# Edge weights scaled in PSUM a group ahead, in place of gathered rows scaled at their landing

## What is computed

```python
h = jax.nn.silu(edge_length_embedded @ W_fc1 * (1.0 / math.sqrt(N_BASIS)))
w = h @ W_fc2 * (1.0 / math.sqrt(N_HID))
w1, w2, w3, w4 = (w[:, 0 * MUL:1 * MUL], w[:, 1 * MUL:2 * MUL], w[:, 2 * MUL:3 * MUL], w[:, 3 * MUL:4 * MUL])
x0s = y0[edge_src]
x1s = y1[edge_src]
ea0 = edge_attr[:, :1]
ea1 = edge_attr[:, 1:]
mid0a = w1 * x0s * ea0
mid0b = w4 * jnp.einsum('eum,em->eu', x1s, ea1) * (1.0 / math.sqrt(3.0))
mid1a = (w2 * x0s)[:, :, None] * ea1[:, None, :]
mid1b = w3[:, :, None] * x1s * ea0[:, None, :]
edge_features = jnp.concatenate([mid0a, mid0b, mid1a.reshape(E, -1), mid1b.reshape(E, -1)], axis=1)
agg = jax.ops.segment_sum(edge_features, edge_dst, num_segments=N)
```

## Time and profile before

| | us |
|---|---|
| median of 3 runs | 4927.12 |
| lowest, highest | 4906.59, 4927.83 |
| span of the profiled execution | 4361.2 |
| tensor pass in it, first gather to last sums | 116.8 to 1278 |
| busy in the whole span: PE, DVE, ACT, POOL | 3150.7, 2326.6, 1273.1, 2831.6 |
| mean granted TensorE clock | 0.861 |

### The profile page before, as it was taken

One profiled execution on the slowest core, in us unless ns is written; L12 is line 12 of the kernel. 1 busy time (PEld: TensorE's weight loads), 2 busy tenths in 40 slices (PEclk: granted clock), 3 DMA queues, 4 the chain that ended last, 5 costly groups with the idle time before them and its releaser, 6 DMA issues. The chain is left out here.

```text
span 4361.2 us, 67130 instructions
## 1 busy us (share of the span) xinstructions
PE 3150.7 (72%) x22048; PEld 2138.5 (49%) x22049; DVE 2326.6 (53%) x7490; ACT 1273.1 (29%) x2767; POOL 2831.6 (65%) x2851
## 2 busy tenths in 40 slices
PE   2677777777677888764534457987888688886886
PEld 1666665666555555432322244555555455554444
DVE  5677777777655666666657772335232432324223
ACT  1334344444434444434332240003111121112112
POOL 2777776666534767546747756764777577774775
PEclk8899999999988998975555568998999899997998
DMA  5324455667963444304444558764888578885876
GB/s 181 85 68 96 76 97 91 90 101 102 119 125 88 121 117 116 93 22 85 80 93 79 99 102 266 243 205 156 266 265 262 168 247 263 262 265 168 263 242 181
DMA packets 470576, 659.32 MB, mean 151 GB/s; under 512 B 108665, under 2 KB 335266, under 8 KB 469462
## 3 DMA queue, kind: packets, MB, share of 16 engines
q1 hardware_dynamic: 356438, 377.29, 34.7%
q0 software_dynamic: 113792, 277.69, 24.2%
HBM read 542.27 MB, written 112.46 MB: 150 GB/s over the span
## 5 line engine op out<-in xcount | busy, mean ns | idle before, releaser
L1716 POOL DMA_INDIRECT pass_rows<-table_sage,src_idx x1136 | 1087.0, 957 | 366.7 <-issue 336.7
L1154 POOL DMA_INDIRECT pass_rows<-table_tensor,src_idx x784 | 797.0, 1017 | 350.6 <-issue 223.9
L1775 PE MATMUL pass_dense_ps<-x 128*128 128x512 f16 x2352 | 544.9, 384 | 28.9 <-DMA x<-table_sage 27.9
L2653 POOL DMA_INDIRECT sort_rows<-table_sort,slot_idx x392 | 398.1, 1016 | 183.4 <-issue 118.6
L1382 POOL DMA_INDIRECT pass_rows<-table_gate,src_idx x338 | 331.7, 981 | 174.5 <-issue 96.6
L1775 PE MATMUL pass_dense_ps<-rb 128*128 128x512 f16 x2058 | 424.2, 361 | 25.9 <-DMA rb<-table_sage 24.3
L1837 DVE TENSOR_TENSOR pass_scaled_sums<-pass_sums_ps,rc 128x54 f32<-128x54 f32 (+18 forms) x340 | 60.7, 220 | 577.9 <-PE pass_sums_ps L1800 540.7
L1775 PEld LDWEIGHTS pass_dense_ps<-x 128*128 128x128 bf16 x2352 | 220.7, 99 | 275.7 <-DMA x<-table_sage 28.7
L2567 PE MATMUL pass_counts_ps<-rc 128*128 128x512 bf16 (+13 forms) x1064 | 239.8, 344 | 149.0 <-ACT re L2600 100.5
L1800 PE MATMUL pass_sums_ps<-pass_hot,pass_rows 128*128 128x68 bf16 (+18 forms) x5472 | 214.3, 193 | 162.8 <-DMA pass_rows<-table_sage,src_idx 151.2
L1233 PE MATMUL pass_sums_ps<-pass_hot,pass_prod_a 128*128 128x128 f32 x1568 | 236.4, 298 | 120.0 <-DVE ra L1248 96.7
(11 more groups left out here) (379 smaller groups left out, 6108.9 us busy)
## 6 DMA issues: line engine op xcount, KB each, us to landing
rb<-dense SPq DMA_DIRECT2D x98, 512.0 KB
x<-dense SPq DMA_DIRECT2D x196, 256.0 KB
x<-table_sage SPq DMA_DIRECT2D x196, 192.0 KB
dense<-re SPq DMA_DIRECT2D x11, 3136.0 KB, 26.1
rb<-dense SPq DMA_DIRECT2D x98, 296.0 KB
pass_counts<-dense SPq DMA_DIRECT2D x98, 256.0 KB
rb<-table_sage SPq DMA_DIRECT2D x196, 96.0 KB
table_sage<-x SPq DMA_DIRECT2D x24, 768.0 KB
```

The lines of the kernel that those rows point to most:

```text
L1154: nc.gpsimd.indirect_dma_start(rows[:, h, t, :], None, table, bass.IndirectOffsetOnAxis(ap=idx[:, at:at + 1], axis=0)).then_inc(gathered[h ...
L1716: nc.gpsimd.indirect_dma_start(rows[:, h, t, :], None, table, bass.IndirectOffsetOnAxis(ap=idx[:, at:at + 1], axis=0)).then_inc(gathered[h ...
L1775: ins = nc.tensor.matmul(dense_ps[:, a * most_cols + at:a * most_cols + to], table_ring[:, k, from_table:from_table + P], counts_ring[:, k ...
L2653: nc.gpsimd.indirect_dma_start(rows[:, b, j, :], None, table, bass.IndirectOffsetOnAxis(ap=slot_idx[:, at:at + 1], axis=0)).then_inc(gathe ...
```

## The change

ACT no longer scales the gathered rows. Instead it scales, in place in PSUM, the two of four weight channels that `ea0` belongs to (w1 and w3, 64 of 128 columns per tile), as soon as PE has made them, one group before they are used. `a_scalars` and `a_vectors` then read the gathered rows themselves. ACT's list becomes: hidden layer of q+2, scaling of the weights of q+1, evictions of q. DVE waits for the scaled weights (`weighed`) at its second product, where it waited for the weights, and no longer waits for ACT at `a_scalars`. The buffer `y_ea0` is gone.

```diff
         def _(act):
-            def silu(q, r):
-                if holds_back(q - 1):
+            def silu(q):
+                if q >= 2:
                     act.wait_ge(weight_made, q - 1)
                 act.wait_ge(hidden_summed, q + 1)
...
-                    silu(q + 1, (h + 1) % 2)
-                    if holds_back(q - 1):
-                        act.wait_ge(operands_made, q - 1)
-                    act.wait_ge(gathered[h], gathers.count(h, GROUP_TILES * (i + 1)))
-                    for t in range(GROUP_TILES):
-                        ins = nc.scalar.activation(y_ea0[:, r, t, :], rows[:, h, t, :], ACT.Copy,
-                                                   scale=cols(extra["edge_attr"], (q * GROUP_TILES + t) * 4, 1))
-                    ins.then_inc(ea0_made, 1)
+            def weigh(q):
+                act.wait_ge(weight_made, q + 1)
+                for t in range(GROUP_TILES):
+                    scaled = weight_ps[:, q % 2, t * P:(t + 1) * P].rearrange("p (c u) -> p c u", u=MUL)[:, 0:4:2, :]
+                    ins = nc.scalar.activation(scaled, scaled, ACT.Copy,
+                                               scale=cols(extra["edge_attr"], (q * GROUP_TILES + t) * 4, 1))
+                ins.then_inc(weighed, 1)
...
+            silu(0)
+            silu(1)
+            weigh(0)
+            for q in range(GROUPS):
+                silu(q + LOOK)
+                if q + 1 < GROUPS:
+                    weigh(q + 1)
+                for t in build.turns(q, BUILD_TURNS):
+                    for w in build.ended(t):
+                        build.evict(act, w)
...
-                m = TensorMath(nc, GROUP_TILES, weight_ps[:, r, :], rows[:, h, :, :], y_ea0[:, r, :, :],
+                m = TensorMath(nc, GROUP_TILES, weight_ps[:, r, :], rows[:, h, :, :], rows[:, h, :, :],
...
-                dve.wait_ge(weight_made, q + 1)
+                dve.wait_ge(weighed, q + 1)
                 m.y0_weighed().then_inc(step, 1)
                 dve.wait_ge(step, 3 * q + 1)
                 m.dot_first().then_inc(step, 1)
-                dve.wait_ge(ea0_made, q + 1)
                 m.a_scalars()
```

More of the change, by code:

```diff
@@ L1107, in tensor_pass @@
         hidden = s.sb("hidden", [HID, 2, GROUP_TILES * P])
-        y_ea0, y_ea1 = s.sb("y_ea0", [P, 2, GROUP_TILES, P]), s.sb("y_ea1", [P, GROUP_TILES, 3, MUL])
+        y_ea1 = s.sb("y_ea1", [P, GROUP_TILES, 3, MUL])
         w2_y0, dot = s.sb("w2_y0", [P, GROUP_TILES, MUL]), s.sb("dot", [P, GROUP_TILES, 2, MUL])
@@ L1111, in tensor_pass @@
             extra["room"].rearrange("p (r t f) -> p r t f", r=2, t=GROUP_TILES)
-        ea0_made, step, dotted, emptied = s.sem("ea0_made"), s.sem("step"), s.sem("dotted"), s.sem("hot_emptied")
+        weighed, step, dotted, emptied = s.sem("weighed"), s.sem("step"), s.sem("dotted"), s.sem("hot_emptied")
         hidden_ps, weight_ps = s.ps("hidden", [P, 512]), s.ps("weight", [P, 2, 512])
@@ L1165, in _ @@
         def _(act):
-            def silu(q, r):
-                if holds_back(q - 1):
+            def silu(q):
+                if q >= 2:
                     act.wait_ge(weight_made, q - 1)
                 act.wait_ge(hidden_summed, q + 1)
-                nc.scalar.activation(hidden[:, r, :], hidden_ps[0:HID, :], ACT.Silu,
+                nc.scalar.activation(hidden[:, q % 2, :], hidden_ps[0:HID, :], ACT.Silu,
                                      scale=1.0 / math.sqrt(BASIS)).then_inc(hidden_made, 1)
[L1173 to L1177, removed]
-                    silu(q + 1, (h + 1) % 2)
-                    if holds_back(q - 1):
-                        act.wait_ge(operands_made, q - 1)
-                    act.wait_ge(gathered[h], gathers.count(h, GROUP_TILES * (i + 1)))
-                    for t in range(GROUP_TILES):
-                        ins = nc.scalar.activation(y_ea0[:, r, t, :], rows[:, h, t, :], ACT.Copy,
-                                                   scale=cols(extra["edge_attr"], (q * GROUP_TILES + t) * 4, 1))
-                    ins.then_inc(ea0_made, 1)
-                    for t in build.turns(q, BUILD_TURNS):
-                        for w in build.ended(t):
-                            build.evict(act, w)
-            act.wait_ge(extra["split_stored"], 16 * SPLIT)
-            for i in range(ITERS):
-                body(i)
+            def weigh(q):
[5 more added lines that the diff above has]
+                ins.then_inc(weighed, 1)
+            act.wait_ge(extra["split_stored"], 16 * SPLIT)
+            silu(0)
[8 more added lines that the diff above has]
+                        build.evict(act, w)
         @block.tensor
```

## The result

The changed kernel takes 4936.01 us (median of 12 runs, 4916.51 to 4956.84), the kernel before beside it 4911.48 us (median of 12). The ratio is 1.0055, with a 95% interval of 1.0037 to 1.0073: slower, by about 27 us. The forecast was 4920 us, 7 us faster. The time lies just inside the range, but by luck: the kernel before ran 16 us faster in these runs than in the three from which the forecast was made. Counted as a difference, the range is -25 to +11 us, and +27 lies outside it. The direction is wrong.

What follows compares the result with a forecast made beforehand. POOL's gather issue was taken to bound the tensor pass, 1020.9 of 1143 us, leaving at most 122.4 us to win. -4.6 - 2 + 0 = -6.6 us on 4927.1 gave about 4920 us, range 4902 to 4938.

Steps and rivals of the forecast that it cites:

- the short waits: Tensor pass: POOL's 36 short waits for sums, 28 us; claimed net 0, bounds -28 and +18 us.
- later evictions: Tensor pass: evictions behind hidden layer and scalings start 0.5 us later; a third of 36 waits, 12, give +6 us.
- DVE's shorter waits: Where sums wait for DVE's products, DVE no longer stands for ACT: 6 of the other 24 waits, -7.5 us.
- rival 2: PE before a window's first count: late eviction sets the pace of 36 waits; 4956 us at 1 us, chance 0.07.
- 566 us of a run lie outside the profile's span: Whole run: median 4927.1 us against the profile's span of 4361.2 us; the difference was taken as unchanged.
- Rival 1: Ring-limited part of the tensor pass: DVE's wait is the pace, all 28 us go, 4892 us; chance 0.10.
- The late gathers: After eleven late gather landings, DVE's 0.41 us stand for ACT's scalings goes: 11 x 0.42 = -4.6 us.
- the eviction that waits for a store: After an ACT eviction held by a store, PE reaches its counts earlier: -2 us, bounds -2.9 and 0.
- signs named for rival 2: Tensor pass: POOL's waits over 145 us, with PE's wait for evictions well over 200 us.

Runs made afterwards that it cites:

- evictions first: The change with ACT's list turned round to evictions of q, hidden layer of q+2, scalings of q+1; ratio 1.0002 to the kernel before.
- before again: The kernel before, unchanged, profiled again on one chip with the change; span 4968.4 us, time 4970.28 us, median 4954.8 us.
- the change again: The change, unchanged, run again on one chip beside the kernel before; ratio 1.0080 to it.
- first comparison: The change, unchanged, against the kernel before, on another chip than the later runs; 4936.01 against 4911.48 us, ratio 1.0055.
- extra scalings ahead: The change with its evictions put first and four unread 128x64 scalings added ahead of each eviction; ratio 1.0101 to the kernel before.
- the control: The change with its evictions put first and four unread 128x64 scalings added behind each eviction; ratio 1.0001 to the kernel before.
- planned places: The change, offset loaded ahead of the wait, 69 evictions first in ACT's list, 57 behind hidden layer and scalings; ratio 0.9973 to the kernel before.

## Why the prediction was wrong

**The step that failed** is "the short waits", where I set +6 us for later evictions against -7.5 for DVE's shorter waits and took 0. In place of the 0 the runs showed 27 and 40 us (0.55 and 0.80%) lost to the late evictions, and nothing won from DVE's waits; with the evictions first the loss is gone. The mechanism stood there, and as rival 2, with the right place and a chance of 0.07.

- *The delay was sized right, the number of evictions wrong.* I had each eviction 0.5 us later. Start of the eviction less the end of the last count product ahead of it, over the 126 evictions of each trace, is 1.69 us on the mean in before again and 2.28 in the change again: 0.59 more. I charged it to 12 evictions. The loss is 27 us by the first comparison and 0.8% of 4954.8, 40 us, by the second: 27 / 0.59 to 40 / 0.59, that is 46 to 68 of the 126 in full, an estimate that charges the whole loss to this delay. With the extra scalings ahead the mean is 1.83 us, with them behind 1.34; 126 x 0.49 = 62 us of lateness cost 0.0100 x 4961 = 50 us against the control, a larger share. So a late eviction has no fixed price, and the mean doesn't order the kernels: with the planned places it is 2.06 us, and no time is lost.
- *Why 12:* I counted in a profile where POOL waits 49 times, 122.4 us, and 0.3 us up to 410 us. In before again it waits 143 times, 280.4 us, of them 52.2 us in 116 to 410. The profile showed far fewer waits than before again has; they were no shorter, 2.5 and 2.0 us on the mean. "566 us of a run lie outside the profile's span, and I leave them as they are" was the assumption behind it, and it was false. Rival 2's own price, a threshold of 0.87 us for each of 36 waits, fails by the same count: the change is slower by 0.55% and 0.8% with 0.59.
- *What DVE's shorter waits give:* nothing, where I set -7.5 us. The wait went, as forecast, and DVE then waited for PE's sums; with evictions first it came back whole, 96.4 us, and with the extra scalings behind it was 151.2, at no cost that the runs can tell. Rival 1 needed just these waits to be the pace; it is out.
- *The late gathers (-4.6) and the eviction that waits for a store (-2)* can't be seen one by one. The kernel with evictions first holds the first of them, at 1.0002 (0.9988 to 1.0016), which is -6 to +8 us. They are not shown.
- *Right:* POOL's busy time and issue gaps are unchanged (786.0 and 198.3 us in the change's first profile, 790.9 and 197.4 in before again); DVE's wait for the scalings is 3.5 to 10.1 us. The scalings take 295 ns (forecast about 320), the four 0.90 us together where I took 0.98:

```profile
L1179 ACT ACTIVATE pass_weight_ps<-pass_weight_ps,rd 128x64 f32<-128x64 f32 x784 | 176.4, 295 | 1.1 <-issue 1.1
```

- *The signs named for rival 2* (POOL's waits over 145 us, PE's wait for evictions well over 200) both came. But the first of them holds for before again too (280.4 us); only the second tells the two kernels apart, 237.6 us against 139.0. Limits taken from the short execution were of little use.

## What to carry to other kernels

Ahead of an instruction that another engine stands still for, nothing goes into its queue that could go behind it: 0.9 us of work cost 1.0% of the time ahead of 126 evictions, and behind them nothing that the runs can tell from zero. A wait that an edit removes is worth time only if the engine isn't held elsewhere at once; here 71 us of DVE's 92.6 turned into a wait for sums. And before a profile is used for sums, its span is held against the timed runs: if they differ by a tenth, its waits are those of another execution.

## What the runs showed of the hardware

- The spans of two profiled executions of one program differ by 607 us. The kernel before took a span of 4361.2 us in its first profile and 4968.4 in its second (on which chip the first was taken isn't known); that one and the 11 other profiles of the study, of whatever kernel, have spans within about 2 us of a time over 4900. DVE and POOL are as busy in the one as in the other (2326.6 and 2336.8 us, 2831.6 and 2839.0), PE is busier in the second (3150.7 and 3380.1 us, at a mean granted clock of 0.861 and 0.822); the rest is idle time. In the second, ACT's hidden layers wait 119.3 us for signals that come after the recorded end of the product they need; among the waits of the first, none of the tensor pass is of this kind ("remote"). Bytes moved are the same, 659.32 MB, at 151 GB/s over the one span and 133 over the other. What holds the signals up stays open.
- ACT's price by where it reads and writes, all 128x64 with a per-partition operand: 295 ns from PSUM to PSUM (above), 321 from PSUM to SBUF, and 335 from SBUF to SBUF, the extra scalings of the control:

```profile
L2609 ACT ACTIVATE pass_pad<-rd 128x64 f32<-128x64 f32 x504 | 131.9, 335 | 0.0
```

- That is 40 ns between the two scalings; they are the same function, but the one in PSUM goes over two runs of 32 columns and the other over one of 64. The 321 ns are those of a sigmoid with a bias (as the 367 ns, from which I took 26 ns for PSUM as a source, are those of a bias added without scaling), so a split into 14 for the source and 26 for the destination isn't shown. The Trainium skill (Perfetto Trace Analysis, "Optimizing Scalar/DVE Operations") has an access overhead of ScalarE of about 93 ns in SBUF and 51 in PSUM, 42 apart, and a profiled latency of about twice that. The durations here differ by about the single amount, when both sides are moved, not by the double one.
